# A vision tower's load order, its convolution pieces, and where the second image's convolution runs

## What is computed

```python
patches = im.reshape(b, c, hp, P, wp, P)                      # 256 patches of 32*8*8 = 2048 values
x = jnp.einsum('bchpwq,dcpq->bhwd', patches, conv_w)
x = x.reshape(b, hp * wp, -1) + conv_b                        # 256 tokens x 128
for i in range(2):
    y = _ln(x, ln1_g[i], ln1_b[i])
    q, k, v = jnp.split(y @ qkv_w[i], 3, axis=-1)             # 8 heads of 64
    q = softmax(q, axis=-1) * scale;  k = softmax(k, axis=-2) # k's over the tokens
    x = x + (q @ (k.T @ v)) @ out_w[i] + out_b[i]             # by head
    x = x + gelu(_ln(x, ...) @ ff1_w[i] + ff1_b[i]) @ ff2_w[i] + ff2_b[i]
h = _ln(x) @ head_w + head_b
h = h + attention(layernorm(h), W_qkv, W_out, b_out)          # W_qkv is the "aqkv" weight
h = h + ffn(layernorm(h), mixed w_fc, mixed w_proj)           # masks from alpha_e, alpha_r
```

## Time and profile before

| | |
|---|---|
| median of three runs | 135.79 us |
| lowest, highest | 134.62, 137.22 us |
| span of the profiled execution | 133.6 us |
| TensorE busy | 120.1 us (90%) |
| VectorE, ScalarE, GpSimd busy | 80.4, 64.4, 48.6 us |
| loaded from HBM | 11.65 MB |

### The profile page before, as it was taken

How to read it: one execution, slowest core, us unless ns; L and a number is a source line. 1 busy time by engine, 2 the same in 40 slices (tenths; PEclk the granted TensorE clock), 3 DMA queues, 4 the chain that set the end, 5 groups by cost and what they waited for, 6 DMA issues and landing times.

```text
span 133.6 us, 2182 instructions
## 1 busy us (share of the span) xinstructions
PE 120.1 (90%) x820; PEld 104.1 (78%) x820; DVE 80.4 (60%) x239; ACT 64.4 (48%) x153; POOL 48.6 (36%) x60
## 2 busy tenths in 40 slices
PE   6979989999999798994999999779889988998992
PEld 6979979976887696982968799668667777996991
DVE  6000366968687954599599887265868478177002
ACT  3000263555496475554483819916583734423520
POOL 0000024061995842349029483256608220052000
PEclk9999999999999999998699999999999999999999
DMA  4999899999000000000000000000000000000101
GB/s 120 359 428 380 284 429 359 351 414 373 6 0 0 0 2 5 0 0 0 0 0 0 0 5 0 0 0 0 7 0 0 0 0 0 5 0 2 59 0 59
DMA packets 3884, 12.18 MB, mean 91 GB/s; under 512 B 441, under 2 KB 1817, under 8 KB 3618
## 3 DMA queue, kind: packets, MB, share of 16 engines
q1 hardware_dynamic: 3874, 12.05, 24.1%
HBM read 11.65 MB, written 0.39 MB: 90 GB/s over the span
## 4 chain that ended last, share of the span: by engine, by line
PE 54%; DVE 13%; issue 9%; DMA 9%; ACT 8%; SPq 3%; POOL 2%; POOLq 1%; DVEq 0%; ACTq 0%
DMA norm_rows_sb<-in_norm_rows 9%; PE bank L394 4%; PE bank L413 4%; PE bank L375 4%; PE bank L319 3%; PE bank L340 3%; PE bank L352 3%; PE bank L382 3%; PE bank L499 3%; DVE xn L947 3%; SPq L261 3%; PE bank L365 3%; PE bank L388 2%; PE bank L328 2%; PE bank L401 2%
## 5 line engine op out<-in xcount | busy, mean ns | idle before, releaser
L1785 POOL TENSOR_TENSOR rstd<-mv,minus_half 128x2 f32<-128x2 f32 x14 | 10.0, 713 | 41.1 <-DVE mv L934 40.7
L1803 POOL TENSOR_TENSOR qn<-q,rqsum 128x512 f32<-128x512 f32 x8 | 8.3, 1044 | 17.8 <-DVE rqsum L994 17.8
L1523 ACT ACTIVATE kexp<-bank,nkmax 128x256 f32<-128x256 f32 x16 | 7.4, 469 | 7.3 <-DVE nkmax L974 5.7
L1564 ACT ACTIVATE patches_sb<-bank,fcb 128x256 f32<-128x256 f32 x12 | 5.1, 469 | 10.6 <-PE bank L496 10.6
L413 PE MATMUL bank<-restw,hid 128*128 128x128 f32 x64 | 8.8, 281 | 1.0 <-ACT hid L1538 1.0
L499 PE MATMUL bank<-projw,patches_sb 128*128 128x192 f32 x48 | 9.3, 330 | 0.0
L319 PEld LDWEIGHTS bank<-embed_sb 128*128 128x128 f32 x64 | 7.9, 198 | 1.5 <-DMA embed_sb<-in_embed 1.5
L319 PE MATMUL bank<-embed_sb 128*128 128x128 f32 x64 | 8.4, 285 | 0.7 <-DMA embed_sb<-in_embed 0.7
L413 PEld LDWEIGHTS bank<-restw,hid 128*128 128x128 f32 x64 | 7.8, 191 | 1.6 <-ACT hid L1538 1.4
L394 PEld LDWEIGHTS bank<-cw,qT 128*128 128x128 f32 x64 | 8.0, 191 | 1.3 <-issue 1.0
L394 PE MATMUL bank<-cw,qT 128*128 128x128 f32 x64 | 8.8, 282 | 0.0
(11 more groups left out here) (168 smaller groups left out, 351.5 us busy)
## 6 DMA issues: line engine op xcount, KB each, us to landing
embed_sb<-in_embed SPq DMA_DIRECT2D x3, 768.0 KB, 7.7
patches_sb<-in_patches SPq DMA_DIRECT2D x2, 1024.0 KB, 12.4
restw<-in_rest_w SPq DMA_DIRECT2D x2, 768.0 KB, 16.0
qkvw<-in_qkv_w SPq DMA_DIRECT2D x3, 256.0 KB, 11.3
qkvw<-in_qkv_w SPq DMA_DIRECT2D x1, 768.0 KB, 15.4
fcw<-in_fc_w SPq DMA_DIRECT2D x1, 768.0 KB, 17.2
embed_sb<-in_embed SPq DMA_DIRECT2D x1, 576.0 KB, 4.1
aqkvw<-in_aqkv_w SPq DMA_DIRECT2D x1, 576.0 KB, 11.9
```

The costliest lines, as they stand in the source:

```text
L1523: return nc.scalar.activation(kexp[:, c, :], K_BANK[s][c // 2][:, (c % 2) * TOKENS:(c % 2 + 1) * TOKENS], ACT.Exp, bias=nkmax[i][:, c:c + ...
L1564: return nc.scalar.activation(hid3[i][:, c, :], src, ACT.Gelu_apprx_tanh, bias=fcb[:, c:c + 1])
L1785: return nc.gpsimd.tensor_tensor(rstd[i][:], mv[i][:, :, 1], minus_half[:], ALU.pow)
L1803: return nc.gpsimd.tensor_tensor(qn[:, t, :].rearrange("p (h d) -> p h d", h=HEADS), q[:, t, :].rearrange("p (h d) -> p h d", h=HEADS), rq ...
```

## The change

SP's queue: embed in ten pieces (chunks 0; 1; 2-3; 4-5; 6-7; 8-9; 10-11; 12-13; 14; 15) with one semaphore each, the bias behind the first; the norm row directly behind embed; image 1's patches in three pieces (4, 4 and 8 chunks), the first ahead of k's weight, the other two behind q's weight and ahead of headw and aqkvw; mix ahead of the second norm row; and the late weights in another order. The bias is loaded as one row (half a KB instead of 64), and its product has one row of ones against it; it is done for both tiles behind the first chunk, and the last chunk signals `conv_done`. TensorE does not warm up between pieces and has three warm-ups behind image 0's convolution. Of image 1, chunks 0 to 2 and the bias run before y's transpose, chunk 3 behind it, then, behind k and q, chunks 4 to 7, 8 to 11 and 12 to 15, with the transposes of kexp between them. On VectorE the low part of k's weight is made ahead of the two operations that give y. ScalarE's and GpSimd's lists are unchanged.

```diff
--- before.py
+++ after.py
@@ -51,7 +51,8 @@
     _at += _n
 NROW = _at
 GROW = 2 * D
-CONV_AT = (0, 1, 4, 8, 12, KCONV)
+CONV_AT = (0, 1, 2, 4, 6, 8, 10, 12, 14, 15, KCONV)
+PATCH_AT = (0, 4, 8, KCONV)
 CONV_PIECES = len(CONV_AT) - 1
 
 
@@ -78,7 +79,7 @@
             at = P + KVW + COL[name][0] + n
             return small_sb[:, at:at + 1]
 
-        convb_sb = sb("convb_sb", [P, D])
+        convb_sb = sb("convb_sb", [1, D])
         norm_rows_sb = [sb(f"norm_rows_sb{l}", [P, GROW]) for l in range(LAYERS)]
         embed_sb = sb("embed_sb", [P, KCONV, D + TOKENS])
         patches1_sb = sb("patches1_sb", [P, KCONV, TOKENS])
@@ -211,9 +212,10 @@
         FC3_BANK = [(bank[3], bank[2], bank[6]), (bank[5], bank[0], bank[0])]
 
         loaded = {n: sem(f"loaded_{n}") for n in (
-            "aout", "aqkv", "cb", "embed0", "embed1", "embed2", "embed3", "embed4", "fc", "head",
-            "mix", "patches1a", "patches1b", "proj", "qkv0k", "qkv0q", "qkv1", "rest0", "rest1",
+            "aout", "aqkv", "cb", "fc", "head", "mix", "proj", "qkv0k", "qkv0q", "qkv1", "rest0", "rest1",
             "rg", "rows", "small", "v0")}
+        loaded_embed = [sem(f"loaded_embed{n}") for n in range(CONV_PIECES)]
+        loaded_patches = [sem(f"loaded_patches{n}") for n in range(len(PATCH_AT) - 1)]
         aqkv_weight_high, attention3_columns, attention3_ready, attention3_turned, attention_done, centred1 = (
             sem(n) for n in ("aqkv_weight_high", "attention3_columns", "attention3_ready", "attention3_turned", "attention_done", "centred1",))
         centred3, centred_last, coefficients_ready, context3_done, context3_ready, context_block_ready_act = (
@@ -260,39 +262,40 @@
             def load(dst, src, name):
                 sp.dma_start(dst, src).then_inc(loaded[name], 16)
 
-            def load_embed(first, last, name):
-                load(embed_sb[:, first:last, :], embed0[:, first:last, :], name)
-
-            def load_patches(first, last, name):
-                load(patches1_sb[:, first:last, :], patches1[:, first:last, :], name)
+            def load_embed(n):
+                at = slice(CONV_AT[n], CONV_AT[n + 1])
+                sp.dma_start(embed_sb[:, at, :], embed0[:, at, :]).then_inc(loaded_embed[n], 16)
+
+            def load_patches(n):
+                at = slice(PATCH_AT[n], PATCH_AT[n + 1])
+                sp.dma_start(patches1_sb[:, at, :], patches1[:, at, :]).then_inc(loaded_patches[n], 16)
 
             def store(i, t):
                 sp.dma_start(out[i, :, t, :], outs[i][:, t, :]).then_inc(stored, 16)
 
-            load_embed(0, 1, "embed0")
-            load_embed(1, 4, "embed1")
-            load_embed(4, 8, "embed2")
+            load_embed(0)
             load(convb_sb[:], convb, "cb")
-            load_embed(8, 12, "embed3")
-            load_embed(12, 16, "embed4")
-            load_patches(0, 8, "patches1a")
+            for n in range(1, CONV_PIECES):
+                load_embed(n)
             load(norm_rows_sb[0][:], norm_rows0.to_broadcast([P, GROW]), "rg")
+            load_patches(0)
             load(qkvw[0][:, INNER:2 * INNER], qkv_w[0][:, INNER:2 * INNER], "qkv0k")
             load(small_sb[:], small, "small")
             load(qkvw[0][:, 0:INNER], qkv_w[0][:, 0:INNER], "qkv0q")
+            load_patches(1)
+            load_patches(2)
             load(headw[:], head_w, "head")
             load(aqkvw[:], aqkv_w, "aqkv")
-            load_patches(8, 16, "patches1b")
+            load(mix_sb[:], mix, "mix")
             load(norm_rows_sb[1][:], norm_rows1.to_broadcast([P, GROW]), "rows")
             load(rows_sb[:], rows.to_broadcast([P, NROW]), "rows")
-            load(mix_sb[:], mix, "mix")
             load(qkvw[0][:, 2 * INNER:], qkv_w[0][:, 2 * INNER:], "v0")
+            load(restw[0][:], rest_w[0], "rest0")
+            load(qkvw[1][:], qkv_w[1], "qkv1")
+            load(restw[1][:], rest_w[1], "rest1")
+            load(fcw[:], fc_w, "fc")
+            load(projw[:], proj_w, "proj")
             load(aoutw[:], aout_w, "aout")
-            load(restw[1][:], rest_w[1], "rest1")
-            load(qkvw[1][:], qkv_w[1], "qkv1")
-            load(projw[:], proj_w, "proj")
-            load(fcw[:], fc_w, "fc")
-            load(restw[0][:], rest_w[0], "rest0")
             sp.wait_ge(out_ready, 2)
             store(0, 1)
             store(0, 0)
@@ -317,11 +320,13 @@
                         left = (embed_sb[:, c, D + t * P:D + (t + 1) * P] if i == 0
                                 else patches1_sb[:, c, t * P:(t + 1) * P])
                         mm = nc.tensor.matmul(CONV_BANK[i][t][:, 0:D], left, embed_sb[:, c, 0:D],
-                                              start=(c == 0), stop=False)
-                return mm
-
-            def conv_bias(i, t):
-                return nc.tensor.matmul(CONV_BANK[i][t][:, 0:D], ones[:, 0:P], convb_sb[:], start=False, stop=True)
+                                              start=(c == 0), stop=(c == KCONV - 1))
+                        if c == KCONV - 1:
+                            mm.then_inc(conv_done, 1)
+
+            def conv_bias(i):
+                for t in range(TILES):
+                    nc.tensor.matmul(CONV_BANK[i][t][:, 0:D], ones[0:1, 0:P], convb_sb[:], start=False, stop=False)
 
             def turn(dst, src):
                 for t in range(TILES):
@@ -501,40 +506,22 @@
 
             pe.wait_ge(consts_set, 1)
             warm_up(bank[0], 4)
-            pe.wait_ge(loaded["embed0"], 16)
+            pe.wait_ge(loaded_embed[0], 16)
             conv(0, 0, 1)
-            warm_up(bank[0], 2)
-            pe.wait_ge(loaded["embed1"], 16)
-            conv(0, 1, 2)
-            conv(0, 2, 3)
-            conv(0, 3, 4)
-            warm_up(bank[0], 2)
-            pe.wait_ge(loaded["embed2"], 16)
-            conv(0, 4, 5)
-            conv(0, 5, 6)
-            conv(0, 6, 7)
-            conv(0, 7, 8)
-            pe.wait_ge(loaded["embed3"], 16)
-            conv(0, 8, 9)
-            conv(0, 9, 10)
-            conv(0, 10, 11)
-            conv(0, 11, 12)
-            pe.wait_ge(loaded["embed4"], 16)
-            conv(0, 12, 13)
-            conv(0, 13, 14)
-            conv(0, 14, 15)
-            conv(0, 15, 16)
             pe.wait_ge(loaded["cb"], 16)
-            conv_bias(0, 0).then_inc(conv_done, 1)
-            conv_bias(0, 1).then_inc(conv_done, 1)
-            pe.wait_ge(loaded["patches1a"], 16)
-            conv(1, 0, 2)
-            conv(1, 2, 4)
-            conv(1, 4, 6)
+            conv_bias(0)
+            for n in range(1, CONV_PIECES):
+                pe.wait_ge(loaded_embed[n], 16)
+                conv(0, CONV_AT[n], CONV_AT[n + 1])
+            warm_up(bank[0], 3)
+            pe.wait_ge(loaded_patches[0], 16)
+            conv(1, 0, 1)
+            conv_bias(1)
+            conv(1, 1, 3)
             pe.wait_ge(y_ready, 2)
             pe.wait_ge(loaded["small"], 16)
             turn(TURN1_BANK[0], y[0]).then_inc(y_turned, 1)
-            conv(1, 6, 8)
+            conv(1, 3, 4)
             pe.wait_ge(y_high, 1)
             pe.wait_ge(key_weight_low0, 1)
             k_high(0, 0)
@@ -551,19 +538,17 @@
             k_low(0, 2).then_inc(k_done, 1)
             k_high(0, 3)
             k_low(0, 3).then_inc(k_done, 1)
-            pe.wait_ge(loaded["patches1b"], 16)
-            conv(1, 8, 10)
-            conv(1, 10, 12)
+            pe.wait_ge(loaded_patches[1], 16)
+            conv(1, 4, 8)
             pe.wait_ge(k_exp_ready, 2)
             turn_k(0, 0, 0).then_inc(k_turned, 1)
-            conv(1, 12, 14)
-            conv(1, 14, 16)
-            conv_bias(1, 0).then_inc(conv_done, 1)
+            pe.wait_ge(loaded_patches[2], 16)
+            conv(1, 8, 12)
             pe.wait_ge(k_exp_ready, 4)
             turn_k(0, 0, 1).then_inc(k_turned, 1)
+            conv(1, 12, KCONV)
             pe.wait_ge(coefficients_ready, 1)
             mix_fc_masks()
-            conv_bias(1, 1).then_inc(conv_done, 1)
             pe.wait_ge(q_shifted, 2)
             turn_k(0, 1, 0).then_inc(k_turned, 1)
             turn_k(0, 1, 1).then_inc(k_turned, 1)
@@ -1102,12 +1087,12 @@
             dve.wait_ge(mean1_ready, 2)
             dve.wait_ge(x_ready, 2)
             centre_and_gain(0, 1).then_inc(centred1, 1)
+            dve.wait_ge(key_weight_high, 1)
+            qk_low_part(0, 1).then_inc(key_weight_low0, 1)
             dve.wait_ge(deviation1_ready, 1)
             scale_and_offset(0, 0).then_inc(y_ready, 1)
             dve.wait_ge(centred1, 2)
             scale_and_offset(0, 1).then_inc(y_ready, 1)
-            dve.wait_ge(key_weight_high, 1)
-            qk_low_part(0, 1).then_inc(key_weight_low0, 1)
             dve.wait_ge(query_weight_high, 1)
             qk_low_part(0, 0)
             dve.wait_ge(y_high, 1)
@@ -1939,8 +1924,7 @@
     headmask[:EC, EC:] = np.kron(np.eye(HG, dtype=np.float32), np.ones((D3, 1), np.float32))
```

(3 more changed lines are left out.)

## The result

| | before | after |
|---|---|---|
| median of four runs each, side by side | 135.2 us | 138.98 us |
| lowest, highest | 134.48, 137.22 | 137.44, 140.82 |
| span of the profiled execution | 133.6 | 139.0 |
| ratio, after to before | | 1.018 [1.010, 1.026] |
| medians of a second measurement (after_again, below) | 135.73 | 138.68, span 136.8 |

The change costs some 2.5 to 3 us, about 2%; the interval runs from 1.0 to 2.6%, so whether the loss reaches 2% is not settled. The forecast was 136.8, +1.0. The profiled execution is the slowest of the eight runs of the changed kernel, so after_again is read beside it.

What follows compares the result with a forecast made beforehand. TensorE, busy 90% of the span, was taken as the bound: its block ending at 29.6 instead of 28.55 adds 1.0 us to the 133.6 us span, and 2.2 lie around it, giving 136.8 us, range 135.0 to 138.4.

Steps and rivals of the forecast that it cites:

- The wait: ScalarE waits for aqkvw ahead of k's exponentials, so TensorE waits 0.9 us at the transpose of kexp.
- the landing of aqkvw: Load queue: aqkvw, now behind all patches, lands at 21.9, 2.7 us later than before.
- the transpose that needs them starts at about 24.15: TensorE's first transpose of kexp starts once two exponentials are ready at 24.1; before, it came at 24.27 without waiting.
- three per cent of the 8.4 us: Load queue: embed's ten smaller pieces cost 0.25 us, from 422 against 436 GB/s.
- its two small terms: In aqkvw's landing sum: minus 0.16 us for the smaller bias, plus 0.25 us for embed's small pieces.
- The rival of slow pieces: All of embed loads at 312 GB/s instead of 375, 1.7 us longer: +2.7 us, 138.5; chance 0.10.
- the k and q stage ends at 21.5: TensorE's front: k and q products end at 21.5 instead of 22.48, 1.0 us gained.
- it lands at 16.52 - 1.2 = 15.3: Load queue: the key weight lands at 15.3, with 576 KB less ahead of it, giving y at 17.3.
- the later chunks (+1.15): TensorE after k and q: twelve chunks of image 1 instead of eight, less the bias products, add 1.15 us.
- Even without a wait about +0.1: TensorE's chain: 1.15 us more work less 1.0 gained at the front leaves about +0.1 us.
- the 29.6 of the forecast: TensorE's last transposes of keys end at 29.6 against 28.55, +1.0 us, and all later stages shift with them.
- The clock rival: TensorE's idle times halve its clock once, losing 1.7 us of work: 137.6, or 138.5 behind the exponentials' wait; chance 0.10.

Runs made afterwards that it cites:

- after_again: The changed kernel, unedited, measured a second time: median 138.68 us against 135.73 for the kernel before, 1.022 of medians.
- a_warm: The changed kernel with the four TensorE warm-ups between image 0's convolution pieces put back: ratio 1.018 to the kernel before.
- c_bias_full: The changed kernel with the bias loaded as 128 rows (64 KB) again, its place kept: one run, 136.8 us.
- b_aqkvw_late: The kernel before with aqkvw issued behind the second half of the patches, in large pieces: ratio 0.999 to the kernel before.
- c_y_first: a_late_split with VectorE's order of the kernel before, both y operations ahead of the low part of k's weight: ratio 1.002 to the kernel before.
- a_late_split: The changed kernel with both halves of ScalarE's aqkvw split moved behind image 0's exponentials: ratio 1.0067 to the kernel before.
- b_norm_full: The kernel before with both norm rows laid out 128 times by the host: ratio 0.981 to the kernel before, medians of all its runs 0.990.
- c_norm_full: a_late_split with both norm rows laid out 128 times by the host: ratio 1.001 to the kernel before.

## Why the prediction was right in its mechanism and short in its size

The range of 135.0 to 138.4 took in the result narrowly: 1.018 times 135.79 is 138.2, while the median, 138.98, lies above it. The wait came as forecast, but two steps of the sum failed, the landing of aqkvw by 1.7 to 2.2 us and the front by 1.0, where the whole forecast was +1.0. That the time stayed within the range is in part luck.

**The wait, right.** ScalarE stood for aqkvw (5.0 and 4.5 us), TensorE for kexp, nowhere else longer in the first profile, and everything later moved as one block. The step "the transpose that needs them starts at about 24.15", that is 2.25 us behind the landing, held in four profiles: 24.13 to 26.37, 23.60 to 25.84, 23.52 to 25.76 (a_warm), 23.13 to 25.38 (c_bias_full).

**The landing of aqkvw, mis-sized: 21.9 forecast, 24.1 and 23.6 measured.** The failed term is "three per cent of the 8.4 us", 0.25 us for the small pieces. I took it from one microsecond in mid-queue. Measured from 2 to 10 us, large pieces moved 376 GB/s (b_aqkvw_late; 375 to 381 over five profiles), the ten pieces 330 (after_again; 313 to 345 over nine). (376 - 330) x 8 us is 0.37 MB, at 395 KB/us some 0.9 us instead of 0.25. That is 0.65 of the 1.7 to 2.2 us by which the landing was late. With large pieces and the same bytes ahead of it, it landed at 22.16 (b_aqkvw_late), where the sum without its two small terms has 21.8. The eight profiles with ten pieces and aqkvw behind the patches have it landed at 22.5 to 24.1, 1.1 later in the mean. No run changed the pieces alone, so that they are the cause is argued from these rates and landings and not shown. The spread of 1.6 us among the eight is open: in the first profile head to aqkvw took 2.6 us for 576 KB, in the others 1.4 to 1.6. One premise failed too: that the queue "lands in the order of issue". In after the second norm row was issued at 12.55, behind aqkvw (10.94), and landed at 22.85, ahead of it (24.13); in after_again it landed at 22.81, ahead of 23.60. Whether what is queued behind aqkvw slows it was not tested. The rival of slow pieces was priced at 1.7 us and came true by half. The Trainium skill, "DMA: Bandwidth & Descriptors", section "Bandwidth", says that smaller transfers lose rate, and the direction agrees with these rows; the 240 GB/s that I had estimated from its table, which is of transfers issued from GpSimd, was far too low for this queue, which was never empty (DMA share 0.96).

**The front, wrong: "the k and q stage ends at 21.5".** It ended at 22.5 in both profiles of the changed kernel (24.3, when TensorE began to wait, less a run of 1.78), and the kernel before had ended it at 22.48. The step that failed is "it lands at 16.52 - 1.2 = 15.3" for the key weight: it landed at 16.3. Some 0.7 us of this is the same small-piece term by the rates; the rest (0.3) wasn't traced. Embed's own landing does not show it (11.96 and 12.18, forecast 12.2): the lateness appears behind embed, 0.5 to 0.6 us at the norm row and 1.1 at the first patches. That this weight would come to hold y was forecast, and c_y_first confirms it; y came at about 18.2 for 17.3. So nothing was gained at the front, and the later chunks (+1.15) were left uncovered. In the changed kernel this stayed hidden, since TensorE waited for the exponentials anyway; it shows once that wait is gone. "Even without a wait about +0.1" measured +1.6 in the block of a_late_split, and +1.0 to +1.6 in its time with none or one stretch.

**The sum again, with what was measured.** In after_again: landing +1.7; the block behind it 5.80 long for 5.42, since the first pair of transposes took 0.44 for 0.22, as in all four profiles in which it followed a wait, and the last four 0.60 for 0.45. From 29.57, the 29.6 of the forecast: 29.57 + 1.7 + 0.4 = 31.67, measured 31.64. In the first profile: landing +2.2, block +0.4, half clock +1.6 (2.61 + 2.39 + 0.43 for 1.79 + 1.79 + 0.22), 33.8, measured 33.80.

**The clock rival, partly.** It named a lowered clock behind the wait for the exponentials, at 1.7 us; in the first profile it came there, at 1.6. In after_again, a_warm and c_bias_full, with waits of 1.5, 0.7 and 0.8, it didn't. "Shorter idle times did not do this" fits, but one case doesn't show that the length of the wait decides.

**Smaller steps.** In after, the forecast in brackets: embed landed at 12.0 (12.2), the norm row at 13.9 (13.3), the first patches at 15.7 (14.6). Image 0's convolution ended at 14.9 and 13.1 for 12.7, the first at the lower pace of the front.

## What to carry to other kernels

Where an in-order engine waits for a load with other work behind it, price the load's landing with its own error, and find the landing from which the wait costs: here 22.2 cost nothing, and at 23.6 TensorE waited 1.5 us. Cutting a load into pieces lets work start sooner, and here everything behind it landed later; take its price from a stretch that holds only such pieces. When runs scatter by steps, sort them by granted clock before believing a ratio: four runs, none of them at full clock throughout, made what was probably a real improvement look like none.

## What the runs showed of the hardware

**One row read by 128 partitions.** Its 128 KB load drops the whole queue to 103 and 220 GB/s for two microseconds in before and 123 and 228 in after, elsewhere less deeply (a_late_split 282 and 313); the same stretches ran at 375 to 408 with tiled rows in b_norm_full and c_norm_full. Over 10 to 16 us it is 309 to 356 GB/s in nine profiles against 392 to 401 in five with tiled rows.

**A small VectorE instruction stretched fivefold.** Timelines of after, VectorE and GpSimd:

```profile
24.94 1.39 DVE L1002 TENSOR_SCALAR alpha_eseg<-mix_sb 9x4 f32<-9x4 f32 x1
```

```profile
24.91 1.40 POOL L1773 TENSOR_TENSOR aqkvw_lo<-aqkvw,aqkvw_hi 64x576 fp32r<-64x576 f32 x1 [7.89 <-ACT aqkvw_hi L1498]
```

In before, a_late_split, c_y_first and after_again, where GpSimd's instruction did not overlap it, it took 0.27. Here it ended with GpSimd's, 0.02 apart. The Trainium skill, "SBUF — State Buffer", section "Who interferes with whom", says that VectorE and GpSimd share a pair of ports as an exclusive lock, and these two rows agree. It was off the chain here.

**The clock record starts late.** At the front the granted clock reads 1.00 while weight loads take 333 ns, as they do at a granted 0.50. There the duration of a known instruction is the better clock.
